# Seven rows of a partition side by side in three DRAM tables of a graph kernel, with the source list mapped to that order

## The reference, cut to what matters

```
ZU = einsum('nd,kdr->knr', x, U)                    # 4 heads of 16: 64 floats of a node
logits = (ZU[:, src] * ZU[:, dst]).sum(-1) / 4      # softmax over the edges of each dst
agg    = segment_sum(alpha * ZU[:, src], dst)
x1  = layernorm(x + relu(grad_step(x, agg)))        # dense 256 x 256 work per node
agg = segment_mean(x1[src], dst)
out = layernorm(x1 + (relu(agg @ W_l.T + b_l + x1 @ W_r.T) + x1))
```

## Time and profile before

| | |
|---|---|
| median of 3 runs | 4531.06 us (4528.36 to 4538.78) |
| the profiled execution | 4548.04 us, span from first to last instruction 4545.9 us |
| busy share: PE, DVE, ACT, POOL | 20%, 50%, 17%, 73% |
| start (0 to 337 us) | until POOL begins its gathers without a break |
| first edge stage, first node stage | 337 to 2255 us, 2255 to 2423 us |
| second edge stage, last node stage | 2423 to 4388 us, 4388 to 4546 us |
| DMA | 795.21 MB, 175 GB/s on the mean; full share in the first 180 us, 0.30 to 0.35 in the first edge stage, about 0.65 in the second |

### The profile page before, as it was taken

How to read it: one execution, slowest core, us unless ns; L and a number is a source line. 1 busy time by engine, 2 the same in 40 slices (tenths; PEclk the granted TensorE clock), 3 DMA queues, 4 the chain that set the end, 5 groups by cost and what they waited for, 6 DMA issues and landing times. The chain is left out here.

```text
span 4545.9 us, 42018 instructions
## 1 busy us (share of the span) xinstructions
PE 929.0 (20%) x3091; PEld 612.3 (13%) x3091; DVE 2283.0 (50%) x9500; ACT 783.3 (17%) x1430; POOL 3311.1 (73%) x3504
## 2 busy tenths in 40 slices
PE   7301112111112000000194211122222221112027
PEld 6301101001001000000052100111111110011026
DVE  2107656666565665566573443344343344334348
ACT  2001101001001000000042222222222222222125
POOL 6677777777777777777565777777777777777755
PEclk6555555556556555555576555555555555555569
DMA  9803243333333322223284666666666666666768
GB/s 345 318 27 122 86 132 96 97 121 97 108 110 96 108 80 89 80 80 119 87 262 142 221 207 232 240 240 240 240 220 221 220 212 205 228 240 232 255 221 319
DMA packets 343366, 795.21 MB, mean 175 GB/s; under 512 B 90534, under 2 KB 231051, under 8 KB 313604
## 3 DMA queue, kind: packets, MB, share of 16 engines
q1 hardware_dynamic: 164706, 380.87, 23.5%
q0 software_dynamic: 138064, 277.00, 20.1%
q10 hardware_dynamic: 40274, 134.62, 7.6%
HBM read 420.40 MB, written 371.83 MB: 174 GB/s over the span
## 5 line engine op out<-in xcount | busy, mean ns | idle before, releaser
L559 POOL DMA_INDIRECT sb_big<-x,sb_idx x1549 | 1464.6, 945 | 512.2 <-issue 471.8
L559 POOL DMA_INDIRECT sb_big<-zu_rows,sb_idx x1542 | 1455.9, 944 | 482.6 <-issue 469.6
L1407 DVE SCALAR_TENSOR_TENSOR ps_V<-ps_V,sb_keepc,sb_big 128x256 f32<-128x256 f32 x1518 | 747.7, 493 | 132.5 <-ACT sb_big L998 79.1
L998 ACT COPY sb_big<-ps_V 128x1024 f32<-128x1024 f32 (+1 forms) x414 | 399.5, 966 | 1289.0 <-DVE ps_V L1407 1286.3
L741 PE MATMUL ps_T<-sb_ident,sb_xg 128*128 128x128 f32 x392 | 114.4, 390 | 2409.4 <-ACT sb_tileT L877 1248.4
L1407 DVE SCALAR_TENSOR_TENSOR ps_V<-ps_E,sb_keepc,sb_big 128x256 f32<-128x256 f32 x46 | 22.7, 492 | 1020.5 <-DMA sb_big<-x,sb_idx 980.8
L741 PEld LDWEIGHTS ps_T<-sb_ident,sb_xg 128*128 128x128 f32 x392 | 71.9, 200 | 2467.4 <-ACT sb_tileT L877 1259.6
L1162 DVE TENSOR_TENSOR_SCAN ps_V<-ps_V,sb_big 128x34 f32<-128x34 f32 x2944 | 355.4, 206 | 10.0 <-issue 10.0
L1213 DVE TENSOR_TENSOR_SCAN sb_big<-ps_E,sb_big 128x34 f32<-128x34 f32 x2944 | 355.3, 202 | 1.6
L1170 DVE TENSOR_TENSOR sb_big<-ps_V,sb_big 128x2176 f32<-128x2176 f32 x46 | 111.5, 2423 | 390.6 <-DMA sb_big<-zu_rows,sb_idx 390.6
L559 POOL DMA_INDIRECT sb_hn<-rows,sb_nidx x196 | 189.5, 967 | 69.2 <-issue 52.7
(11 more groups left out here) (237 smaller groups left out, 1838.0 us busy)
## 6 DMA issues: line engine op xcount, KB each, us to landing
rows<-sb_big SPq DMA_DIRECT2D x46, 3072.0 KB, 10.6
rows<-sb_big SPq DMA_DIRECT2D x46, 1280.0 KB, 13.6
rows<-sb_big ACTq DMA_DIRECT2D x46, 1224.0 KB, 5.4
z_at_start<-sb_big ACTq DMA_DIRECT2D x46, 1088.0 KB, 9.6
sb_big<-z_at_start SPq DMA_DIRECT2D x46, 1088.0 KB, 6.4
sb_zx<-zu_rows SPq DMA_DIRECT2D x2816, 0.2 KB
sb_big<-x SPq DMA_DIRECT2D x1920, 1.0 KB
sb_xg<-in_x_dram SPq DMA_DIRECT2D x36, 768.0 KB, 6.4
```

The lines of the kernel that those rows point to most:

```text
L559: pool.indirect_dma_start(to, None, table, bass.IndirectOffsetOnAxis(ap=index.bitcast(U32), axis=0), **more).then_inc(done, 16)
L998: act.copy(slot1[s][:, cols, :], V0[:, first_word:first_word + width].rearrange("p (c f) -> p c f", f=D)).then_inc(col_copied, 1)
L1407: dve.scalar_tensor_tensor(out=sums_at(j), in0=before, scalar=keepc[:, j:j + 1], in1=slot1[s][:, j, :], op0=ALU.mult, op1=ALU.add).then_in ...
```

## The change

Within a group, the row of node (block b, partition p) moves from `g*896 + b*128 + p` to `g*896 + p*7 + b` in `zu_rows`, `x1` and `own`. A partition's seven rows then lie side by side (1792 bytes in `zu_rows`, 7168 bytes in `x1` and `own`). The input x and the output keep their order.

```
+        block_i = regA[:, 0:COLS].bitcast(I32)
+        def side_by_side(dram, g):
+            return dram[bass.ds(g * GN, GN), :].rearrange("(p b) f -> p b f", p=P)
+        HALVES = ((0, P // 2), (P // 2, P))
             def load_group(to, dram, g, done, rows=P):
+                if dram is x1:
+                    for a, b in HALVES:
+                        sp.dma_start(to[a:b], side_by_side(x1, g)[a:b], max_dma_last_dim=4 * D).then_inc(done, 16)
+                    return
...
-                sp.dma_start(node_group(zu_rows, 2 * i + s), zu[:, bass.ds((2 * i + s) * GB, GB), :]
+                sp.dma_start(side_by_side(zu_rows, 2 * i + s), zu[:, bass.ds((2 * i + s) * GB, GB), :]
...
-                sp.dma_start(node_group(own[layer], g), hg[0]).then_inc(bg_stored[layer], 16)
+                sp.dma_start(side_by_side(own[layer], g), hg[0]).then_inc(bg_stored[layer], 16)
...
-                sp.dma_start(yg[u], node_group(own[layer], g)).then_inc(n_loaded[layer][u], 16)
+                sp.dma_start(yg[u], side_by_side(own[layer], g), max_dma_last_dim=4 * D).then_inc(n_loaded[layer][u], 16)
...
-            gather(zcar0[:, :], zu_rows, dst_i[:, 1:2], zcar_loaded)
+            pool.wait_ge(rows_placed, 2)
+            gather(zcar0[:, :], zu_rows, zcar_i[:, 0:1], zcar_loaded)
...
-            act.wait_ge(edges_loaded, 16 * 6)
+            act.wait_ge(rows_placed, 2)
...
+                    if layer == 0:
+                        for a, b in HALVES:
+                            act.dma_start(side_by_side(x1, g)[a:b], normed[s][a:b]).then_inc(n_stored[0][s], 16)
+                        return
...
+            for row, blk, node_of in ((src_i[:, 0:COLS], block_i, src_i[:, 0:COLS]),
+                                      (zcar_i[:, :], zcar_b[:, :], dst_i[:, 1:2])):
+                done(dve.tensor_scalar(blk, node_of, P.bit_length() - 1, None, ALU.logical_shift_right))
+                done(dve.tensor_scalar(row, node_of, P - 1, None, ALU.bitwise_and))
+                done(dve.scalar_tensor_tensor(out=row, in0=row, scalar=float(GB), in1=blk, op0=ALU.mult, op1=ALU.add))
+                done(dve.tensor_scalar(blk, blk, float(NTH), None, ALU.mult))
+                done(dve.tensor_scalar(blk, blk, NTH_BITS, None, ALU.logical_shift_right))
+                dve.scalar_tensor_tensor(out=row, in0=blk, scalar=float(GN - GB), in1=row, op0=ALU.mult, op1=ALU.add
+                                         ).then_inc(rows_placed, 1)
+            dve.wait_ge(rows_placed, 2)
```

More of the change, by code:

```diff
@@ L81, in gnn_kernel @@
     NZ = 4
+    NTH, NTH_BITS = 147, 10
     NX = 4
     assert FP * FQ == NF and FQ * FW <= C * F and CA % GC == 0 and NGC % 2 == 1 and C % GC == 2 and NG * GB == NB and NG % NX == 2 and NCH % S1 == 1 and NCH % 2 == 0 and NG < NCH // S1 and 0 < ELAST <= COLS and NF * FW == E
-    assert E <= EP and D == 2 * P
+    assert E <= EP and D == 2 * P and all(b * NTH >> NTH_BITS == b // GB for b in range(NB))
     zu_rows = nc.dram_tensor("zu_rows", (NP, F), F32, kind="Internal").ap()
@@ L215, in gnn_kernel @@
         zcar0 = sb("zcar0", [P, F])
+        zcar_i = sb("zcar_i", [P, 1], I32)
+        zcar_b = sb("zcar_b", [P, 1], I32)
         scar = sb("scar", [P, F + H])
@@ L269, in gnn_kernel @@
         first_known = sem("first_known"); next_made = sem("next_made"); nodes_known = sem("nodes_known"); z_scattered = sem("z_scattered")
-        zcar_loaded = sem("zcar_loaded")
+        zcar_loaded = sem("zcar_loaded"); rows_placed = sem("rows_placed")
         w_pe = sem("w_pe"); w_dve = sem("w_dve"); w_exp = sem("w_exp")
```

## The result

The changed kernel takes 4546.89 us (median of 8 executions, 4539.71 to 4562.22), before 4530.94 us (8 executions): a ratio of 1.0031, 95% interval 1.0021 to 1.0040. It is slower by 0.3%; the forecast was 4521.6 us.

What follows compares the result with a forecast made beforehand. POOL's 3091 edge gathers at a fixed 1.25 us step were taken to bound the kernel. Start -8.5 and x1 stores -1.0 summed to -9.5 us, from 4531.06 to 4521.6 us; range 4508 to 4535.

Steps and rivals of the forecast that it cites:

- Last node stage: "0": Last node stage: loads have as many 1 KB pieces as before and the output is unchanged, so 0 us.
- Rival C: Node stage: 7 KB pieces of x1 delay gathers, PE stays longer at half clock; slower, 4545 us; chance 0.09.
- The start: 8.5 us: Start, up to the scatter: scatter begins near 201.3 us instead of 209.81, a gain of 8.5 us.
- Its sign of being wrong: Start: the prediction called itself wrong if the scatter still begins after 206 us.
- The working behind the 6: Start: one window's lower GB/s, put on two stores of `zu_rows`, gave 6 us less DMA time for all fourteen.
- whole 7.5 us: Start, index mapping on DVE: by the skill's rule POOL's gathers may lose all 7.5 us; 4 us was taken.
- the zeros are at 207.4 - 6 = 201.4: Start: DMA time saved on `zu_rows` stores brings the zeros 6 us earlier, to 201.4 us, holding the scatter near 201.3.
- a slack of 2 us: Start, kernel before: zeros landed about 207.4 us, some 2 us before POOL asked for them.
- rival A: Start: zeros end hardly earlier, or the mapping blocks POOL throughout; gain 2 to 5 us, 4526 to 4529; chance 0.16.
- Stores of x1: -1.0: First node stage: longer pieces shorten POOL's wait for the last x1 store; between 0 and 2.4 us, 1.0 taken.
- The bound of 2.4: First node stage, x1 stores: most that could be gained, from 33.3 us at 386 GB/s to 30.9 at 411.
- Edge stages: 0: Edge stages: POOL's gathers keep number and size and don't wait for `own` or `x1` transfers, so 0 us.

Runs made afterwards that it cites:

- experiment 1: Changed kernel with x1's loads split by block (0 to 5, 6) over all 128 partitions instead of in halves: 4533.4 us, ratio 0.9983.
- experiment 3: Kernel before, with x1 stored and loaded in two transfers over the lower and upper 64 partitions, old layout: ratio 1.0023.
- experiment 5: Changed kernel with x1's loads and stores split into even and odd partitions instead of lower and upper half: ratio 1.0001.
- experiment 12: On experiment 1, last node stage only: own loaded in lower and upper halves, x1 in one transfer over all partitions: ratio 1.0012.
- experiment 2: Changed kernel with own alone stored and loaded in the layout of before; x1 still side by side and in halves: ratio 1.0028.
- experiment 6: On experiment 1, x1's stores also split by block, so that nothing is in halves: ratio 0.9992.
- experiment 9: Changed kernel with only zu_rows side by side; x1 and own stored and loaded as before: ratio 0.9983.
- experiment 8: On experiment 1, three stores of zeros from behind the node-group loop issued in its last three rounds: ratio 0.9998.
- experiment 10: Experiments 6 and 8 together, x1's loads and stores by block plus three earlier stores of zeros: ratio 0.9986.
- experiment 11: Kernel before, with only three stores of zeros moved into the loop's last three rounds: ratio 1.0031.
- experiment 7: On experiment 1, the 1 KB limit on loads of own and x1 removed: ratio 0.9998.

## Why the prediction was wrong

**Last node stage: "0".** This step decided it. "Its loads have as many pieces of 1 KB as before" is true, and the number of pieces is not their price: with the same pieces the engines took 80.8 us for 64.0, since half of them came in transfers that fill only partitions 0 to 63 or 64 to 127. Experiments 1, 3, 5 and 12 show it by four different edits; all last stages with such loads are 180 to 191 us (five kernels), all others with pieces of 1 KB 168.4 to 169.5 (eight, with before). The waits agree: DVE waits for loads of x1 in the last stage of the changed kernel and of experiments 2, 3 and 12 (4.5 to 9.7 us), and not in before, 1, 5, 6 and 9. The diff shows the halves in two lines, and no rival looked at them. Rival C was slower for another reason, the pieces of 7 KB of x1's stores in the first node stage; that its 4545 us lies 2 us from the measured time is chance, for PE's low stretch from 2342 us on is some 44 us long both before and after.

The Trainium skill, "SBUF — State Buffer", section on the DMA port swizzle, speaks against this change, and the prediction didn't use it: a transfer over partitions 0 to 63 reaches 8 of 16 ports of SBUF, 196 GB/s at 1 MiB against 328 over all 128, and by its section "Can I just issue two DMAs to hit both halves?" the two don't make up for each other. The trace agrees: 217 GB/s at a full share against 360, and even and odd partitions, which by its table reach all 16 ports, run at 360 again. That the ports are the mechanism is the page's word; the runs show which partitions matter, not why.

**The start: 8.5 us.** Its sign of being wrong, a scatter after 206 us, came. Term by term: the stores of `zu_rows` save 4.9 us of DMA time in the loop (forecast 6, right in size). The working behind the 6 was not: it put all 459 KB of two stores, 1792 pieces, into the window 112 to 116 us, but the two took 10.9 us to land (median), and the window has 825 packets of under 512 bytes in all:

```profile
DMA packets 1718, 1.26 MB, mean 315 GB/s; under 512 B 825, under 2 KB 1666, under 8 KB 1703
```

So that term came out by luck. The stores land in 4.4 to 12.2 us, median 6.4 (forecast 4.5), and the last is issued at 149.6 us, 2.6 earlier (forecast 4); POOL no longer waits for them (in experiment 1, with the same start, it does for 4.06 us) and is ready at 200.5 us (forecast 201.1, right). The mapping lengthens POOL's gathers by 4.3 us, 129.8 against 125.5 for the 98 (forecast 4, right). The first three beside DVE's work:

```profile
28.10 2.43 POOL L573 DMA_INDIRECT sb_hn<-in_dst_dram,sb_frow_i  x1 [19.93 <-DVE sb_frow_i L1072]
30.83 1.59 POOL L573 DMA_INDIRECT sb_hn<-in_dst_dram,sb_frow_i  x1 [0.30 <-issue]
32.73 2.53 POOL L573 DMA_INDIRECT sb_hn<-in_dst_dram,sb_frow_i  x1 [0.30 <-issue]
```

and the first of the mapping's two instructions that read two tiles:

```profile
32.34 1.79 DVE L1084 SCALAR_TENSOR_TENSOR sb_src_i<-sb_src_i,sb_big 128x1564 int32<-128x1564 int32 x1
```

DVE's six instructions take 7.5 us as forecast, and POOL loses 4.3. The seven stretched gathers (28.10 to 41.93 us) each end 0.8 to 1.1 us behind the DVE instruction in which they began, close to a gather's own 0.94; the next one, at 43.76 us beside a reduction, takes 0.95 again. So a gather stands at most for the rest of one instruction, and gets through between two. The "whole 7.5 us", which the prediction drew from the Trainium skill, "SBUF — State Buffer", section "Who interferes with whom", did not come.

What failed is "the zeros are at 207.4 - 6 = 201.4". The saved DMA time would reach the zeros only if more of them were issued in it. But the code issues two stores of zeros per group in the loop, and the loop goes at PE's pace, at half clock (PEclk 0.50 in the window of the loop above); it ended 2.6 us earlier, and the zeros about 2. Nor was there a slack of 2 us in that execution of the kernel before, as the prediction read from the earlier trace rows: in the changed kernel POOL's release follows the engines' last work by 1.7 us, and with as much in before the zeros came when POOL did (208.0 + 1.7 = 209.7, POOL done with its gathers at 209.51). The scatter in the nine kernels with `zu_rows` side by side and the zeros in their old place begins at 205.6 to 211.9 us, mean 207.5. That is rival A, "the zeros end hardly earlier", in the place that it had. Its size, 2 to 5 us, fits but isn't fixed: the two executions with the old start have their scatter at 209.81 and 215.66 us (before and experiment 3). Experiments 8 and 10 take the wait for the zeros away (0.30 us is left), and POOL then waits some 4 us for `zu_rows` instead; experiment 11 shows that without zu's longer pieces the same edit costs 9 to 15 us.

**Stores of x1: -1.0.** Not seen. POOL's wait for the last of them is 42.3 us, had 40.4. (The bound of 2.4 is a slip: 12.8 MB at 411 GB/s are 31.2 us and not 30.9, which leaves 2.1.) The DMA time behind the term didn't fall either, and the halves are why: ACT's queue over the stage, before (170 us) and after (172 us), has

```profile
q10 hardware_dynamic: 12992, 12.85, 21.9%
q10 hardware_dynamic: 2240, 12.85, 23.2%
```

which is 37.2 and 39.9 us, where the same pieces of 7 KB over even and odd partitions take 31.4 (experiment 5). The time of the stage shows neither: it goes by PE's clock first of all. A window of the changed kernel (GB/s last, before it DMA share and PEclk):

```profile
2360.00:2380.00 20.00, 20.00 (x42) 10.11 (x42) 10.58 (x33) 6.49 (x14) 11.19 (x13) 0.50 0.75 236
```

and of experiment 5:

```profile
2360.00:2380.00 20.00, 19.81 (x76) 10.80 (x75) 17.54 (x68) 12.81 (x30) 11.20 (x12) 1.00 0.74 253
```

PE is busy in both, and does 42 matmuls at half clock and 76 at full. Profiled executions with over 40 us at half clock took 168 to 170 us for the stage (before, changed, 3, 7, 9 and 10), those with 17 us or less 150 to 155. Among those that were at full clock throughout, but for 3 us, the old layout took 150.1 us (experiment 11, one execution), the new one 152.5 to 153.9 (1, 2, 8 and 12): rather a loss of 2 to 4 us than a gain. Why is open.

**Edge stages: 0.** Right: the first of these waits of POOL shows the same fixed step as the earlier trace rows (the second is the one for x1 that was just named).

```profile
POOL sb_big L573 <- issue: 941.6, 3089, 0.3
POOL sb_big L573 <- DMA x<-sb_big: 42.3, 1, 42.3
```

The +1.0 and +1.8 us of the table are about 1 ns per gather; other kernels with the same lines show +0.9 (experiment 1) and 0.0 (experiment 5) in the second.

With the last stage at +11.3 and the start at -2.1 the two come to +9.1 us, in place of 0 and -8.5; the rest of the +14.2 us is the +2.2 of the node stage and the +2.9 of the edge stages.

Without the halves the change is as fast as before or slightly faster: 0.9983 to 1.0001 over five kernels (1, 5, 6, 8 and 10), of which only experiment 1's interval lies below 1 as a whole. Their mean, 0.9992, is 3.6 us of 4531, in rival A's 2 to 5 us; but two of the five have the earlier zeros as well, and no change of this size is clear of the noise.

## What to carry to other kernels

A load's price is not its pieces alone: keep each transfer spread over all 128 partitions (split a group by columns, or by even and odd partitions, and not by the lower and the upper half), and look in the windows for a full DMA share that moves fewer GB/s. DMA time saved in a loop is worth little to transfers whose number in the loop is fixed: ask who issues the ones that end last. (Moving three of them into the gap took the wait for them away here, and POOL then stood for the next one; no gain in the time was seen.) And a split into halves that is made for the sake of a count of semaphores is a change of its own, to be priced like the rest.

## What the runs showed of the hardware

Loads in halves cost more than their own time: two small transfers beside them each took about 2.4 us longer (waits of 8.72 and 5.26 us in place of 6.37 and 2.78). Stores from halves, with pieces of 7 KB, took 38.6 us of the engines' time instead of 31.4 over even and odd partitions, which the time of the stage did not show. And a limit of 1 KB on the pieces of a load was worth 6.6 us of the last stage by block and 10.5 in halves: with pieces of 6 and 7 KB ACT waited 16.5 and 25.1 us for its own stores of the output, and 0 and 7.3 us with pieces of 1 KB.
